# Causal attention scores: from piecewise maxima in PSUM to whole rows in an SBUF ring, and a later place for the fourth search pass

## The reference, cut to what matters

```
# dense block: 8 heads of 64, causal
attn = einsum('bihd,bjhd->bijh', q, k) * scale
attn = attn * mask - NEG * (1.0 - mask)          # mask = lower triangle
attn = softmax(attn, axis=2)
res  = einsum('bijh,bjhd->bihd', attn, v)
# sparse block: 8 heads of 16, each row keeps its 16 best keys
logits = einsum('bmd,bpd->bmp', q * scale, k)
_, idx = top_k(logits, 16)
attn = softmax(einsum('bmd,bmkd->bmk', q * scale, gather(k, idx)))
out  = einsum('bmk,bmkd->bmd', attn, gather(v, idx))
```

## Time and profile before

| | |
|---|---|
| runs | 4088.46, 4089.54, 4089.97 us (median 4089.54) |
| profiled execution | 4087.79 us, its span 4086.0 us |
| granted TensorE clock, mean of the span | 0.933 of full speed |
| busy: DVE, PE, ACT, POOL | 88%, 84%, 53%, 51% |
| instructions | 88294 |

### The profile page before, as it was taken

How to read it: one execution, slowest core, us unless ns; L and a number is a source line. 1 busy time by engine, 2 the same in 40 slices (tenths; PEclk the granted TensorE clock), 3 DMA queues, 4 the chain that set the end, 5 groups by cost and what they waited for, 6 DMA issues and landing times.

```text
span 4086.0 us, 88294 instructions
## 1 busy us (share of the span) xinstructions
PE 3446.9 (84%) x31480; PEld 2189.8 (54%) x31480; DVE 3587.1 (88%) x5059; ACT 2174.7 (53%) x5587; POOL 2071.6 (51%) x4675
## 2 busy tenths in 40 slices
PE   5997989898998989888898999989897899965555
PEld 4665555655565555655556555655555555633233
DVE  3335999999999999989999999999999999988986
ACT  0774655555655656555555656555554466532222
POOL 2444555645556555655546555565556455553332
PEclk9998999999999999999999999999998899977777
DMA  6105332353235432264224433262323422243332
GB/s 92 23 15 98 66 66 47 74 109 71 49 50 105 86 63 50 45 128 79 47 47 94 87 68 50 47 129 51 60 50 70 85 58 48 45 101 60 64 53 47
DMA packets 915186, 273.20 MB, mean 67 GB/s; under 512 B 877425, under 2 KB 892226, under 8 KB 914754
## 3 DMA queue, kind: packets, MB, share of 16 engines
q1 hardware_dynamic: 902352, 263.99, 35.3%
q10 hardware_dynamic: 12402, 3.56, 0.7%
HBM read 78.86 MB, written 18.67 MB: 24 GB/s over the span
## 4 chain that ended last, share of the span: by engine, by line
PE 35%; DVE 30%; issue 17%; POOL 9%; SPq 4%; ACT 3%; DMA 3%; ACTq 0%; DVEq 0%; POOLq 0%
DVE A L1618 9%; PE bank_ps L1020 6%; DVE M L1631 6%; DVE top L1623 5%; DVE top L1611 5%; PE bank_ps L1137 5%; PE bank_ps L1194 5%; PE score_ps L1109 4%; PE bank_ps L1214 3%; PE bank_ps L1199 3%; POOL PB L957 3%; PE logit_ps L1181 3%; POOL M L987 2%; SPq L843 2%; DVE newmax L1577 2%
## 5 line engine op out<-in xcount | busy, mean ns | idle before, releaser
L1431 ACT ACTIVATE PT<-bank_ps 125x512 f32<-125x512 f32 x1296 | 750.7, 600 | 779.4 <-PE bank_ps L1199 776.9
L1611 DVE MAX8 top<-logit_ps 128x8 f32<-128x1101 f32 x576 | 749.8, 1302 | 92.5 <-PE logit_ps L1181 90.5
L1623 DVE MAX8 top<-A 128x8 f32<-128x1101 f32 x576 | 749.8, 1302 | 6.7
L1618 DVE MATCH_REPLACE8 A<-top,logit_ps 128x1101 f32<-128x1101 f32 x576 | 746.2, 1295 | 0.9 <-issue 0.9
L1631 DVE MATCH_REPLACE8 M<-top,A 128x1101 bf16<-128x1101 f32 x576 | 744.3, 1292 | 0.6 <-issue 0.6
L986 POOL TENSOR_TENSOR top<-top 128x1 f32<-128x1 f32 x576 | 112.3, 195 | 1074.9 <-DVE M L1631 1074.4
L1194 PE MATMUL bank_ps<-stack 128*125 128x512 bf16 (+5 forms) x1728 | 603.8, 365 | 55.5 <-DMA MT<-M 35.6
L987 POOL TENSOR_SCALAR M<-M 128x1000 bf16<-128x1000 bf16 x576 | 591.8, 1027 | 49.7
L1354 ACT ACTIVATE PB<-score_ps,negmax 128x128 f32<-128x128 f32 (+1 forms) x840 | 493.9, 596 | 208.8 <-DVE negmax L1572 162.7
L1181 PE MATMUL logit_ps<-stack 128*128 128x512 bf16 (+1 forms) x1728 | 387.8, 336 | 256.2 <-DVE A L1618 254.3
L1199 PE MATMUL bank_ps<-MT,to_keys 128*125 128x256 bf16 (+7 forms) x2016 | 563.8, 317 | 0.0
(11 more groups left out here) (153 smaller groups left out, 4814.5 us busy)
## 6 DMA issues: line engine op xcount, KB each, us to landing
stack<-qk_parts SPq DMA_DIRECT2D x504, 72.0 KB, 2.9
X<-in_x SPq DMA_DIRECT2D x232, 60.8 KB
qk_parts<-OT SPq DMA_DIRECT2D x16, 864.0 KB, 5.5
X<-in_x SPq DMA_DIRECT2D x232, 57.0 KB
MT<-M SPq DMA_TRANSPOSE x576, 3.2
Wp<-in_L_attn_W_in SPq DMA_DIRECT2D x96, 64.0 KB, 2.0
out<-H SPq DMA_DIRECT2D x8, 512.0 KB
X<-in_x SPq DMA_DIRECT2D x232, 3.6 KB
```

What stands on the lines that cost most here:

```text
L1431: nc.scalar.activation(PT[0:rows, q % P_SLOTS, :], where[0:rows, :], ACT.Exp).then_inc(free(group), 1)
L1611: nc.vector.max(tops_of(n)[:, 0:8], logit_ps[:, 0:L]).then_inc(top8, 1)
L1618: nc.vector.match_replace(A[:, n % 2, :], tops_of(n)[:, 0:8], logit_ps[:, 0:L], NEG).then_inc(cut8, 1)
L1623: nc.vector.max(tops_of(n)[:, 17:25], A[:, n % 2, :]).then_inc(top16, 1)
```

## The change

The scores are copied out of PSUM as they come, piece by piece ("keep_s"): by VectorE for image 0, by ScalarE for the others. They go into a ring `PB` of 2304 columns x 2 heads in SBUF, which takes the place of four slots of 512 columns and a tail. A unit lies in it as one stretch, and before its first piece the copy waits until the last unit that lay there has been turned. GpSimd then masks the diagonal block, VectorE takes one maximum over the unit's rows in SBUF, ScalarE one exponential per head in place, and GpSimd the power -1 of the sums and the scaling. The products with the mask, the events "gap", "correct" and "total", the minima and VectorE's reciprocal are gone. Apart from that, cut of tile t now comes behind strike of tile t+1, and the due time of logits is 10 us earlier.

```diff
+RING = 2304
+def ring_places():
+    place, gone, at, held = [], [], 0, []
+    for u, (_c, _p, i) in enumerate(UNIT):
+        width = min(128 * (i + 1), L)
+        if at + width > RING:
+            at = 0
+        over = [n for n, a, z in held if a < at + width and z > at]
+        place.append(at)
+        gone.append(max(over) if over else None)
...
# planner
-                add("PE", 1.15 * w / 512 + 0.05 + (0.35 if diagonal else 0), due, ("scores", *f),
-                    *([("exp_part", *FILL[m - score_bufs(c)])] if m >= score_bufs(c) else []),
+                add("PE", 1.15 * w / 512 + 0.05, due, ("scores", *f),
+                    *([("keep_s", *FILL[m - score_bufs(c)])] if m >= score_bufs(c) else []),
...
+                add("DVE" if c == 0 else "ACT", 2 * w * 0.00083 + 0.25, due + 1, ("keep_s", *f), ("scores", *f), *prior,
+                    *([("keep_s", *FILL[m - 1])] if m else []))
...
+                    add("POOL", 0.45, due + 2, ("mask", c, p, i), ("keep_s", *f))
+                    add("DVE", 2 * W * 0.00105 + 0.15, due + 2, ("rowmax", c, p, i), ("mask", c, p, i),
+                        *([("exps", *two_ago)] if two_ago else []))
+                    add("ACT", 2 * (W * 0.00083 + 0.35), due + 3, ("exps", c, p, i), ("rowmax", c, p, i),
+                        *([("invert", *two_ago)] if two_ago else []))
+                    add("POOL", 0.2, due + 4, ("invert", c, p, i), ("exps", c, p, i),
...
-            add("PE", 0.65, first, ("logits", c, t), ("stack", c, t // QUARTER), *([("stack_k", 0)] if n == 0 else []),
+            add("PE", 0.65, first - 10, ("logits", c, t), ("stack", c, t // QUARTER), *([("stack_k", 0)] if n == 0 else []),
...
-            add("DVE", 1.38, first, ("cut", c, t), ("second", c, t),
+            add("DVE", 1.38, first, ("cut", c, t), ("second", c, t), *([("strike", c, t + 1)] if t + 1 < TILES else []),
...
# GpSimd
+                    pool.wait_ge(weighed, nth("exps", c, p, i))
+                    nc.gpsimd.tensor_tensor(rinv[:, u % 2, :], rowsum[:, u % 2, :], inverse[:, :], ALU.pow
+                                            ).then_inc(inverted, 1)
+                elif event == "mask":
+                    pool.wait_ge(score_free, FILL_NO[c, p, i, len(pieces(i)) - 1] + 1)
+                    diagonal = unit(c, p, i)[:, :, 128 * i:]
+                    nc.gpsimd.affine_select(out=diagonal, in_=diagonal, compare_op=ALU.is_ge, fill=MASK, base=0,
+                                            pattern=[[0, 2], [-1, diagonal.shape[-1]]], channel_multiplier=1
+                                            ).then_inc(masked, 1)
...
# ScalarE
+                elif event == "keep_s":
+                    act.wait_ge(score_done, FILL_NO[(c, *of)] + 1)
+                    if j == 0 and RING_GONE[UNIT_NO[c, p, i]] is not None:
+                        gone = UNIT[RING_GONE[UNIT_NO[c, p, i]]]
+                        filled(act, ("turn_causal", *gone, len(groups(gone[2])) - 1))
+                    nc.scalar.copy(unit(c, p, i)[:, :, a:z], scores_of((c, *of))[:, :, 0:z - a]).then_inc(score_free, 1)
...
# VectorE
+                    dve.wait_ge(masked, nth("mask", c, p, i))
+                    if u >= 2:
+                        dve.wait_ge(weighed, nth("exps", *UNIT[u - 2]))
+                    nc.vector.reduce_max(negmax[:, u % 2, :], unit(c, p, i), AX.X, negate=True).then_inc(rowmax, 1)
```

More of the change, by code:

```diff
@@ L81 @@
 QUARTER = TILES // 4
-PB_SLOTS = 4
+RING = 2304
 PT_SLOTS = 4
@@ L357, in make_plan @@
-                add("ACT", 2 * (w * 0.00083 + 0.46), due + 2, ("exp_part", *f), ("rowmax", *f), *prior,
-                    *([("exp_part", *FILL[FILL_NO[f] - 1])] if FILL_NO[f] else []),
-                    *([("invert", *two_ago)] if two_ago else []))
-                if diagonal:
[L361 to L367, removed]
+                if j == 0 and RING_GONE[u] is not None:
+                    gone = UNIT[RING_GONE[u]]
+                    prior = [("turn_causal", *gone, len(groups(gone[2])) - 1)]
@@ L949, in _ @@
                 elif event == "scale":
                     p, i = of
-                    s, J = UNIT_NO[c, p, i] % 2, len(pieces(i)) - 1
+                    s = UNIT_NO[c, p, i] % 2
                     pool.wait_ge(inverted, nth("invert", c, p, i))
[L953 to L958, removed]
+                    w = unit(c, p, i)
@@ L959, in _ @@
+                    for hh in range(2):
+                        last = nc.gpsimd.tensor_scalar(w[:, hh, :], w[:, hh, :], rinv[:, s, hh:hh + 1], None, ALU.mult)
                     last.then_inc(scaled, 1)
@@ L1109, in _ @@
                         last = nc.tensor.matmul(score_v[:, hh, 0:z - a], qk[rows, 0, 128 * i:128 * i + 128],
-                                                qk[rows, 1, a:z], start=True, stop=not diagonal)
-                    if diagonal:
-                        d = 128 * i - a
-                        for hh in range(2):
-                            last = nc.tensor.matmul(score_v[:, hh, d:z - a], ident_b[:, :], mask_b[:, 0:z - a - d],
-                                                    start=False, stop=True)
+                                                qk[rows, 1, a:z], start=True, stop=True)
                     last.then_inc(score_done, 1)
@@ new lines, in _ @@
+                elif event == "keep_s":
+                    p, i, j = of
+                    dve.wait_ge(score_done, FILL_NO[(c, *of)] + 1)
+                    if j == 0 and RING_GONE[UNIT_NO[c, p, i]] is not None:
+                        gone = UNIT[RING_GONE[UNIT_NO[c, p, i]]]
+                        filled(dve, ("turn_causal", *gone, len(groups(gone[2])) - 1))
+                    a, z = pieces(i)[j]
+                    nc.vector.tensor_copy(unit(c, p, i)[:, :, a:z], scores_of((c, *of))[:, :, 0:z - a]
+                                          ).then_inc(score_free, 1)
+                elif event == "rowmax":
```

152 lines of the change are left out of this document (36 added, 116 removed).

## The result

| | before | changed |
|---|---|---|
| median, us | 4089.0 (4085.94 to 4089.97, 4 runs) | 4392.15 (4389.71 to 4399.92, 4 runs) |
| ratio to before | | 1.0746, 95% interval 1.0727 to 1.0765 |
| start of the first search, us | 371.5 | 463.8 |
| seven periods, us (mean of one) | 3274 (467.7) | 3514 (502.0) |
| last image, first to last "first" | 404 | 374 |

The account below looks back on a forecast made before the run. It took TensorE to bound the start, then VectorE's own time plus its waits. Seven periods -118, last image -25 and start -5 sum to -148: 4087.8 down to 3940 us, range 3865 to 4040.

Parts of the forecast that it names:

- A wait that comes: Seven periods: VectorE's maxima wait for GpSimd's masks, 0.1 us each, 25 us, bounds 0 and 260; GpSimd's load stays.
- the fourth: Rival, 7%: GpSimd's queue stops VectorE's maxima, 260 instead of 25 us, 4175 us; decides from 0.69 us a maximum.
- the logits: VectorE's waits for TensorE's logits fall by 42 of 60 us in the periods and 25 of 30.5 in the last image.
- The power: On GpSimd, taken at 0.2 us from a product of the same shape, with nobody on VectorE waiting for it.
- The start: Before the first period TensorE loses 72 mask products, 10.5 us; 5 us gain taken, bounds -5 and 10.5.
- rival 3: The ring, 6%: ScalarE stands still 8.5 us, 28 times, until an older unit is turned; a third reaches VectorE, 4019 us.
- Maxima from SBUF: VectorE's maxima cost the same reading SBUF as PSUM; no difference taken, judged by MAX8's equal 1.31 us on both.
- Last image: The last image's search, without a partner, falls from 405 to 380 us, 25 of its 30.5 us of logits waits going.
- The reciprocals: Leaving VectorE in the seven periods, 252 of them at 0.12 us, worth 30 us.
- the sums' wait: VectorE's wait for row sums in the periods passes to GpSimd, worth 15 us.
- the waits for scores: VectorE's waits for scores in the periods pass to ScalarE, which now copies into the ring, worth 26 us.
- The 7 us: Seven periods: a loss on VectorE from dependent neighbouring passes, 69 us after against 62 before, as fewer maxima separate them.

Follow-up runs that it names:

- e6_reciprocal_back: e1_two_op with the reciprocal on VectorE again in place of GpSimd's power, the plan told 0.16 us for it: 3982.81 us, 0.9732.
- e8_power_told: e1_two_op with the planner told 0.74 us instead of 0.2 for GpSimd's power: 3942.08 us, 0.9637.
- e1_two_op: The changed kernel with the second operation (times 1.0) restored to GpSimd's scaling, the order of all engines untouched: 3969.97 us, 0.9704.
- e5_big_ring_first: e1_two_op with a ring of 4608 columns for image 0 only, the second half lying in PT: 3946.24 us, 0.9643.
- e3_cut_before: The kernel before with only the move of the fourth pass and logits due 10 us earlier: 3966.19 us, 0.97.
- e4_plan_told: The changed kernel with its slow scaling, the planner told the real prices of scaling and power, only orders changing: 4143.96 us, 1.0133.
- e9_both: e5_big_ring_first and e8_power_told together: scaling restored, longer ring for image 0, power's price told: 3929.61 us, 0.96.
- e10_scale_told: e9_both with the planner told 0.84 ns a column and 0.26 us an instruction for the scaling: 3918.24 us, 0.9579.

## Why the prediction was wrong

**The step that failed** is in "A wait that comes": GpSimd "loses 64 small operations and 48 scalings" and its load, "255 of 468 us, stays where it is". It was 343 of 502 us a period (2399.86 / 7). The scalings were counted by their number and taken at the old price, and the dropped second operation was not seen as another form with a price of its own; the trace of before had only the form with two. It takes 2.5 instead of 0.84 ns a column. The Trainium skill, "GPSIMD Engine Reference", section "3.1 Elementwise — side-by-side cycle accounting", says: "For k ≤ 2 the body is RD/WR-port-bound at 1.03 cyc/elem". If k is the number of operations on an element, which the page does not spell out, leaving one out would change nothing. The form with two operations agrees (0.84 ns, where 1.03 of the page's 1.2 GHz cycles are 0.86, an estimate); the form with one, at three times that, does not.

**The rival that came** is the fourth, GpSimd's queue in front of the maximum. It was to decide from 0.69 us a maximum; 206.8 us of masks' waits over the periods' 252 maxima are 0.82. Its mechanism was right, with other things in front of the mask: not one L987 (1.03 us) but a power of 0.72 and two scalings of up to 3.1 us each. The masks' wait itself came 53 us below the 260 that the rival gave it. Its price of 4175 was too low for what it left at the forecast: the same queue held up TensorE's turns, so the logits behind them lost 112 us where the forecast gained 42, and the start came late.

**The power** was taken at 0.2 us from a product of the same shape; it takes 0.72. With the cheap scaling that length costs little: the kernel is no faster with the reciprocal on VectorE (e6_reciprocal_back). That the plan does not know it costs 28 us (e8_power_told against e1_two_op), in part perhaps by the order found. **The mask**, taken at 0.4, takes 0.413.

**The start** was to be 5 us earlier and came 92 later. With the cheap scaling it is 30 later, and e5_big_ring_first shows that these are the ring's waits: rival 3 in another place, on VectorE's own copies in image 0, where the prediction looked only at ScalarE.

**Right, once the form is set aside** (e1_two_op, or the changed kernel where it says so):
- Period 452 us (forecast 451), by luck as far as the parts go, see below. VectorE busy 59 us less in the changed kernel's periods; 62 was named, and the sum's own terms give 60. In e1_two_op, with the same number of its instructions, it is 82 less, so this figure also moves with the waits.
- Maxima from SBUF cost the same. Over 1024 columns one took 1.20 us from PSUM in the kernel before (first row) and from SBUF in the changed kernel (second):

```profile
2572.66 1.20 DVE L1572 TENSOR_REDUCE negmax<-score_ps 128x2 f32<-128x1024 f32 x1
2814.07 1.20 DVE L1548 TENSOR_REDUCE negmax<-PB 128x2 f32<-128x1024 f32 x1
```

- Last image 374 us against 380 forecast; its wait for logits is 3.6 us in place of 30.5.
- Masks waited for 15.1 us in the periods, where 25 were taken.

**Right in sum, not in its parts**: the logits give 12 us in e1_two_op, not 42; with the two planner lines alone (e3_cut_before) they give 40. The reciprocals give 8 to 13, not 30 and the sums' wait, or 41 where the plan knows the power's price (e8_power_told, with what its order gives by chance). That the moved pass alone brings the periods down by 83 us in e3_cut_before, twice its 40 us of logits, was not forecast: VectorE's busy time there is 24 us lower, and the waits for scores are 8.4 us instead of 26.2, which the prediction put down to the ring. Its traces show where the busy time went: the neighbours of which one needs the other's result are 121, 128 and 104 before and 117, 14 and 18 in e3_cut_before, 32 us less at the prediction's 0.21, 0.12 and 0.20 us (an estimate). The 7 us that the prediction charged for them hold for the changed kernel's order only. The Trainium skill, "VectorE: DVE Perf Modes", section "The DRAIN you can't avoid", which the prediction sets against this term, also says that a next operation that is not "held" (the page's word) starts earlier. So the 1.21 us without a wait do not by themselves contradict it.

**Open**: why the form with one operation takes three times as long; and how much of the 174 us between e4_plan_told and e1_two_op (202 against e8_power_told) an order better than the planner's could hide. Neither was tried.

## What to carry to other kernels

An instruction that loses an operand or an operation is a new form: look for a row of that very form before its price is taken over, and where there is none, bound it from both sides like any unknown. An engine that is busy 50% and feeds an in-order queue is not free: three times the price of a step on it cost the whole gain while its share reached only 64% of the span, 68% of the periods. And a change made of two parts is best timed in halves, since here two planner lines alone gave all that the parts gave together, until the plan's prices and the ring at the start were mended as well.

## What the runs showed that was not expected

- GpSimd's product of a tensor and a per-partition scalar takes 0.84 ns a column with a second operation (times 1.0) and 2.5 ns without it: 692 against 1570 ns for 512 columns, 1186 against 3095 for 1101.
- GpSimd's power on 128x2 takes 0.71 to 0.72 us, where the product of that shape takes 0.195.
- A mask of 2x128 columns takes 0.413 us there, where 128 take 0.293.
- A change of the plan's prices by at most 0.24 us a unit moves seven periods by 20 us, in one profiled execution of each kernel (e9_both, e10_scale_told).
